# Class counts of a graph-convolution kernel taken from ScalarE's accumulator instead of VectorE's

## The reference

```python
h = jnp.maximum(_layernorm(x, axis=-1), 0.0)          # x: (32, 256, 1024)
x = x + _L0_gnn_ref(h, adj, b1, adj, b2)              # weights W1 = W2 = adj (256, 256)

def _L0_gnn_ref(x, W1, b1, W2, b2):
    adj = _construct_adj(x, 8)
    h = relu(_gc(swapaxes(x, 1, 2), adj, W1, b1))
    return swapaxes(_gc(h, adj, W2, b2), 1, 2)

def _construct_adj(x, k):
    fv = x.mean(axis=1)                               # one value for each node
    nf = fv / norm(fv)
    sim = nf[:, :, None] * nf[:, None, :]             # an outer product
    _, idx = top_k(sim, k + 1)
    idx = idx[..., 1:]
    adj = zeros((B, N, N)).at[b_ix, r_ix, idx].set(1.0)
    adj = maximum(adj, swapaxes(adj, 1, 2))
    adj = adj.at[:, d, d].set(1.0)
    return adj

def _gc(x, adj, W, b):
    deg = adj.sum(axis=2, keepdims=True)
    return einsum('bij,bjh->bih', adj / deg, x @ W.T + b)
```

## Time and profile before

| what | value |
|---|---|
| median of three runs | 550.68 us (550.3 to 552.01) |
| profiled execution, its own time | 548.81 us |
| its span | 546.9 us |
| PE busy (matmul) | 443.5 us, 81% |
| DVE busy | 435.2 us, 80% |
| ACT busy | 262.8 us, 48% |
| POOL busy | 195.1 us, 36% |
| mean granted TensorE clock | 0.984 of full speed |
| HBM traffic | 34.17 MB read, 33.55 MB written, 124 GB/s over the span |

### The profile page before, as it was taken

The page is one execution under the profiler, slowest core; times in us unless marked ns, Lnnn a source line. Parts: engine busy times, 40 slices in busy tenths (PEclk is TensorE's granted clock), DMA queues, the critical chain, the costliest instruction groups (busy, mean ns, idle before and its releaser), DMA issues.

```text
span 546.9 us, 7292 instructions
## 1 busy us (share of the span) xinstructions
PE 443.5 (81%) x2152; PEld 201.7 (37%) x2188; DVE 435.2 (80%) x788; ACT 262.8 (48%) x548; POOL 195.1 (36%) x873
## 2 busy tenths in 40 slices
PE   1002049999899979998899979998999899999995
PEld 0000024444344434443444434443444344444442
DVE  3857965899979997999789997999799955773362
ACT  2665345754575337741675457534773264004300
POOL 1122535171534425261607153443526250514100
PEclk9999997999899999999899999998999999999999
DMA  8960000006710574037600870067303410131034
GB/s 284 410 271 0 1 0 1 1 2 226 265 49 0 210 240 167 0 113 257 247 1 2 307 278 30 2 221 250 146 1 128 181 77 1 77 155 77 1 136 172
DMA packets 18807, 68.20 MB, mean 125 GB/s; under 512 B 1744, under 2 KB 2384, under 8 KB 18768
## 3 DMA queue, kind: packets, MB, share of 16 engines
q1 hardware_dynamic: 18768, 67.73, 33.8%
HBM read 34.17 MB, written 33.55 MB: 124 GB/s over the span
## 4 chain that ended last, share of the span: by engine, by line
PE 53%; DVE 32%; POOL 6%; ACT 3%; issue 3%; DMA 1%; SPq 0%; POOLq 0%
PE ps L337 42%; DVE xs L780 8%; DVE hl L767 5%; PE ps L349 5%; DVE bn L745 5%; PE pf L362 3%; ACT hf L465 2%; PE pm L385 2%; DVE kind L812 1%; DVE fv L807 1%; DVE onehot L819 1%; POOL nw L554 1%; PE pm L393 1%; ACT hl L474 1%; DVE l2w L866 1%
## 5 line engine op out<-in xcount | busy, mean ns | idle before, releaser
L337 PE MATMUL ps<-hl,wh 128*128 128x512 f16 x1024 | 311.1, 386 | 15.9 <-DVE xs L780 15.8
L337 PE MATMUL ps<-hl,wl 128*128 128x512 f16 x512 | 197.3, 385 | 0.0
L337 PEld LDWEIGHTS ps<-hl,wh 128*128 128x128 f16 x1024 | 98.9, 100 | 142.2 <-DVE xs L780 22.7
L773 DVE SCALAR_TENSOR_TENSOR hl<-ps,hl 128x1024 f16<-128x1024 f32 x64 | 78.2, 1222 | 50.6 <-ACT hl L486 50.1
L465 ACT ACTIVATE hf<-xs,nbias,rstd 128x1024 f32<-128x1024 f32 x64 | 79.1, 1237 | 80.7 <-POOL nbias L564 80.4
L486 ACT ACTIVATE hl<-ps 128x512 f16<-128x512 f32 x128 | 74.9, 590 | 76.8 <-PE ps L349 76.7
L767 DVE TENSOR_TENSOR hl<-hf,hl 128x1024 f16<-128x1024 f32 x64 | 77.4, 1210 | 19.3 <-ACT hl L474 19.2
L780 DVE SCALAR_TENSOR_TENSOR xs<-ps,sc,xs 128x1024 f32<-128x1024 f32 x64 | 80.0, 1262 | 9.0 <-PE ps L349 8.8
L745 DVE BATCH_NORM_STATS2 bn<-xs 128x6 f32<-128x512 f32 x128 | 82.0, 681 | 4.4 <-DMA xs<-x_dram 4.4
L337 PEld LDWEIGHTS ps<-hl,wl 128*128 128x128 f16 x512 | 50.8, 99 | 62.7 <-issue 4.0
L474 ACT ACTIVATE hl<-hf 128x1024 f16<-128x1024 f32 x64 | 67.6, 1057 | 2.0
(11 more groups left out here) (117 smaller groups left out, 391.4 us busy)
## 6 DMA issues: line engine op xcount, KB each, us to landing
xs<-x_dram SPq DMA_DIRECT2D x64, 512.0 KB, 7.0
out_dram<-xs SPq DMA_DIRECT2D x32, 1024.0 KB, 5.0
wt<-adj_t_dram SPq DMA_DIRECT2D x1, 256.0 KB, 4.4
b1r<-b_row_dram SPq DMA_DIRECT2D x1, 128.0 KB, 5.5
b2r<-b_row_dram SPq DMA_DIRECT2D x1, 128.0 KB, 5.8
cs<-consts_dram SPq DMA_DIRECT2D x1, 86.5 KB, 4.2
b<-b_dram SPq DMA_DIRECT2D x1, 1.0 KB, 4.1
```

Source lines behind the costliest of these rows:

```text
L337: pe.matmul(ps[i % 3][:, m], w[:, k, o], hl[:, slot, part, k, cols], start=(k == 0 and w is wh and part == 0), stop=False)
L773: dve.scalar_tensor_tensor(hl[:, n % NHL, 1, :, cols], ps[place(1, n, half) % 3][:], 0.0, hl[:, n % NHL, 0, :, cols], ALU.max, ALU.subtrac ...
```

## The change

`classes` no longer accumulates: it is a plain comparison with the same input and output. The count is taken on ACT by a new function, `class_count`: a copy of the one-hot rows (1024 bf16 to f16) whose accumulator output is count. Its main output goes to the tile kind, whose contents are no longer needed then. A new semaphore, count_ready, tells DVE. `class_counts` leaves its place right behind `classes` and stands behind `rows_x` and `h_lo`, ahead of `rows_t`. On ACT `class_count` stands behind the second h chunk and ahead of `split_rows`; only for the first group (g = -1) it stands ahead of the first h chunk.

```diff
+            def class_count(g):
+
+                act.wait_ge(onehot_ready, g + 1)
+                act.activation(kind[:], onehot[:, g % 2], ACT.Copy, accum_out=count[:]).then_inc(count_ready, 1)
...
+                    if q == 3 and is_group(g + 1) and g < 0:
+                        class_count(g + 1)
                     make_h(n, 0)
...
                     if q == 3 and is_group(g + 1):
+                        if g >= 0:
+                            class_count(g + 1)
                         split_rows(2 * (g + 1))
...
             def classes(g):
                 dve.wait_ge(topk, TK * (g + 1))
-                dve.tensor_scalar(onehot[:, g % 2], kind[:], cs[:, C_WANT:C_WANT + 1], None, ALU.is_equal,
-                                  ALU.add, accum_out=count[:]).then_inc(onehot_ready, 1)
+                dve.tensor_scalar(onehot[:, g % 2], kind[:], cs[:, C_WANT:C_WANT + 1], None, ALU.is_equal
+                                  ).then_inc(onehot_ready, 1)
 
             def class_counts(g):
-                dve.wait_ge(onehot_ready, g + 1)
+                dve.wait_ge(count_ready, g + 1)
                 dve.tensor_scalar(cr[:, 0:64], cs[:, C_PICK:C_PICK + 64], count[:], None, ALU.mult
                                   ).then_inc(cr_ready, 1)
...
                 if to:
                     classes(g + 1)
-                    class_counts(g + 1)
...
                 h_lo(n, 0)
+                if to:
+                    class_counts(g + 1)
                 if to:
                     rows_t(2 * (g + 1))
```

More of the change, by code:

```diff
@@ L208, in gnn_kernel @@
         onehot_ready = sem("onehot_ready")
+        count_ready = sem("count_ready")
         cr_ready = sem("cr_ready")
```

## The result

The changed kernel takes 543.82 us (median of four runs, 543.15 to 544.67) against 550.49 us (550.27 to 552.01) before: a ratio of 0.9874, with a 95% interval of 0.985 to 0.9898, so 5.6 to 8.3 us less. The forecast was 545.4 us and a gain of 5.3. The profiled execution took 543.15 us; its span is 541.2 us, 5.7 less than the span before.

The account below looks back on a forecast made before the run. The kernel was taken as bound by PE and DVE in turn. Six stretches of 0.91 us, less 0.2 us at the start, give 5.3 us: median 545.4 us from 550.68, range 543.2 to 548.5 us.

Parts of the forecast that it names:

- Removed and put in its place on DVE: On DVE, one-hot plus accumulator read, 1.32 us, give way to a plain comparison of 483 ns, 748 at the f32 rate.
- Gain in a stretch: DVE's one-hot stretch on the chain gains 0.91 us in each of groups 1 to 6; group 7 gains zero.
- ACT's copy: Copy and accumulator read cost ACT 1.24 us, hidden in its 3.91 us idle before rows_x; cost zero.
- PE: Waits: 0.2 to 0.3 us before class_sizes, about 0.9 before the next group's first unit, 1.49 before times_q1 unchanged.
- Load: Image load read by stats behind the one-hot keeps 0.4 us to spare; if late, up to 0.5 us in 5 stretches.
- (a): Rival: DVE's one-hot goes at the f32 rate; gain 3.6 us, median 547.0 us; chance 0.08.
- (b): Rival: the image load takes over behind the one-hot, 2.5 us given back, median 547.9 us; chance 0.07.
- Group 0: At the start, DVE's saving is worth nothing; the plain one-hot holds up POOL's gather, 0.2 us lost (0 to 0.48).
- the sum: Whole kernel: 6 x 0.91 = 5.5 us, less 0.2 us, gives a gain of 5.3 us.
- Clock: Fall behind times_q1 costs 1.6 us; change leaves that wait, a run may have one fall more or fewer.
- Rival (d): Clock falls after PE's wait for POOL in all six groups: 8.0 us lost, median 553.4 us; chance 0.03.

Follow-up runs that it names:

- e3: Changed kernel with the class marks held in f32 instead of f16, so the one-hot reads 4-byte elements; 543.76 us, ratio 0.9899 to the kernel before.
- e2: Changed kernel with the two writes of cr back right behind the one-hot, so DVE waits for ACT's copy; 555.29 us, ratio 1.0091 to before.
- e9: Changed kernel with ACT's class_count ahead of the first h chunk in every group; 561.01 us, ratio 1.0215 to the kernel before.
- e8: Changed kernel with the two halves of each image loaded in the other order from image 12 on; 548.62 us, ratio 0.9972 to before.
- e11: Changed kernel with the accumulating one-hot and no ACT copy in group 0 alone; 542.66 us in one run.
- e5: Kernel before with unread matmuls in PE's waits, 8 behind the fourth unit and 6 ahead of times_q1; 547.2 us, ratio 0.9945 to before.
- e4: Changed kernel with the two writes of cr on POOL instead of DVE; 544.22 us, ratio 0.9892 to the kernel before.
- e1: Kernel before with only the two writes of cr moved behind h_lo, the one-hot still accumulating on DVE; 548.25 us, ratio 0.9961 to before.
- e12: Kernel before with 8 unread matmuls in the longer PE wait alone, none ahead of times_q1; 550.25 us, ratio 0.9996 to before.
- e6: Changed kernel with unread matmuls in PE's waits, 4 behind the fourth unit and 6 ahead of times_q1; 540.25 us, ratio 0.9817 to before.
- e7: Changed kernel with the writes of cr on POOL and 4 and 6 unread matmuls in PE's waits; 540.66 us, ratio 0.9822 to before.
- e10: Changed kernel with cr writes on POOL and PE's waits filled, but 20 matmuls ahead of group 0's times_q1; 537.36 us, ratio 0.9758 to before.

## Why the prediction was right, point by point

- **Removed and put in its place on DVE.** The plain one-hot was taken at 483 ns and takes 477; at f32 input taken at 748 and measured 744 (e3). Both ends of the estimate, made from three rows of other shapes, held.
- **Gain in a stretch.** 0.91 us forecast, 0.93 measured, in six groups; group 7 gave nothing.
- **ACT's copy.** 1.24 us forecast, 1.06 + 0.19 measured, hidden; e2 and e9 show that this rests on both the place where the count is read and the place where it is taken.
- **PE.** Wait ahead of class_sizes 0.3 us (0.2 to 0.3 forecast), ahead of the first unit 0.95 (0.9), ahead of times_q1 1.49 (unchanged).
- **Load.** Not late, but with 0.5 us left (rivals (a) and (b) did not come true; e8, with waits of 0.7 to 1.3 us in five stretches, lost 4.6 us in the distances).
- **Group 0.** 0.2 us lost beside POOL's copies, shown by e11. The distance from group 0 to group 1 gave back 0.32 us, which the sum had at nothing; the kernel with the move alone gives back as much (63.41 us against 63.77), so it comes with the move. Here the rule of the Trainium skill (SBUF — State Buffer, Who interferes with whom) agrees with the runs.
- **Clock: the mis-sized term.** The sum was 5.3 us; the spans give 5.7 and the timed medians 6.7. I took the distance of 1.9 us between the profiled execution and the median of the runs over to the changed kernel as a constant, and held that the change leaves the number of falls as it is. It was not a constant: the changed kernel's median lies 0.7 us over its profiled execution, and both profiled executions had one fall of 1.7 us on the chain. Filling its waits gives the kernel before 3.0 us (e5), so its timed runs seem to lose more to falls than that one execution shows. The prediction also counted one fall in six groups and passed over two more in the same trace, in the first units from 140 and 375 us, which cost nothing there. The range allowed one fall more or fewer, and that held the result, 0.6 us above the range's lower end. That much is luck: the DVE time was priced right, but nothing in the prediction said how many falls the timed runs would have. Rival (d), more falls, went the other way.

## What to carry to other kernels

Where two engines bound a kernel in turn, price an instruction by the distance between starts in a gapless row of the engine that ends last there, and check each cover (the gap, what reads the result, the next load) by its own row: the same copy on a half idle engine cost 0, 1.3 to 1.5 or 2.1 us a group by its place and by where its result is read. When a difference comes near to the price of one fall of TensorE's clock, compare undisturbed groups inside single executions, since medians hid 1.5 us in one pair (changed and e4) and added 1.4 in another (before and e1). And waits of PE of 1.5 us and more ahead of long matmul work can be filled with matmuls that nobody reads. Here both waits filled gave 3.0 us (e5), somewhat less than half of what the change gave, and the longer one filled alone gave nothing (e12).

## What the runs showed of the hardware beyond this

- A fall of TensorE's clock from 2.4 to 1.2 GHz came behind a wait of PE of 1.5 us in some groups and not in others of the same execution. It cost 1.7 us where PE ended last behind it and nothing where PE waited afterwards (139.64 to 144.36 us in before). With waits cut to 0.2 and 0.3 us none came between group 1 and PE's last matmul in the one profiled execution of each of e5, e6, e7 and e10; e3 had none there either, with its waits of 1.5 us.
- A mean granted clock of a run is no measure of its loss: 0.976 against 0.985 made no difference in time (before and e12), 0.985 against 0.991 made 2.8 us by the ratios (e12 and e5).
- The plain comparison of DVE with 1024 elements takes 477 ns with f16 input and 744 ns with f32, and its accumulating form 1269 ns with f16. The plain one delayed the eight copies of POOL beside it (2.35 us with f16 and 2.60 with f32 input, e3), the accumulating one did not (2.10 us, e11).
